# Expert stages of a four-layer block: pad rows and expert sums spread over other slots, and the loads of the sums issued six slots later

## The reference

```python
probs = softmax(x @ gate_weight.T)                 # 32 experts
top_vals, top_idx = top_k(probs, 8)
rw = top_vals * (cumsum(renormed top_vals) < 0.8)  # at most 7 of the 8 are kept
rw = rw / sum(rw)
for each expert e:
    g, u = split(x @ gate_up[e].T)                 # 256 -> 2 * 96
    out += (silu(g) * u) @ down[e].T * share_of_e  # 96 -> 256
```

## Time and profile before

| what | value |
|---|---|
| median of the runs shown | 1091.12 us |
| the profiled execution | 1090.43 us |
| its span, first to last instruction | 1088.7 us |
| TensorE busy | 877.9 us, 81% |
| GpSimd busy | 642.1 us, 59% |
| VectorE busy | 583.0 us, 54% |
| ScalarE busy | 544.2 us, 50% |
| mean granted TensorE clock | 0.911 of full speed |

### The profile page before, as it was taken

How to read it: one execution, slowest core, us unless ns; L and a number is a source line. 1 busy time by engine, 2 the same in 40 slices (tenths; PEclk the granted TensorE clock), 3 DMA queues, 4 the chain that set the end, 5 groups by cost and what they waited for, 6 DMA issues and landing times. The chain is left out here.

```text
span 1088.7 us, 20645 instructions
## 1 busy us (share of the span) xinstructions
PE 877.9 (81%) x5504; PEld 665.9 (61%) x5504; DVE 583.0 (54%) x2104; ACT 544.2 (50%) x1084; POOL 642.1 (59%) x636
## 2 busy tenths in 40 slices
PE   5999998971489899999368998988758998999940
PEld 4666665641388699998233443544327887999830
DVE  4566785775373222226776488765535522222665
ACT  6333446640145455555268776766423554556520
POOL 2466648787577777775730010373754777777770
PEclk9999999995599999999679998988887999999975
DMA  9600002162578887773540110135326888778776
GB/s 335 252 1 2 1 20 91 67 240 78 168 233 301 281 267 220 222 259 123 174 136 35 34 35 35 49 121 215 116 103 200 261 303 280 227 218 255 270 243 204
DMA packets 93231, 181.64 MB, mean 167 GB/s; under 512 B 18985, under 2 KB 73788, under 8 KB 92736
## 3 DMA queue, kind: packets, MB, share of 16 engines
q1 hardware_dynamic: 68544, 114.19, 32.7%
q0 software_dynamic: 24576, 66.13, 16.7%
HBM read 96.34 MB, written 92.27 MB: 173 GB/s over the span
## 5 line engine op out<-in xcount | busy, mean ns | idle before, releaser
L1304 POOL DMA_INDIRECT result_rows<-ys,result_slots x288 | 286.6, 995 | 88.0 <-issue 81.0
L989 POOL DMA_INDIRECT expert_rows<-route_rows,index x224 | 223.0, 996 | 87.1 <-issue 68.0
L1955 ACT ACTIVATE b_probs<-ps 128x1024 f32<-128x1024 f32 x128 | 127.9, 1031 | 42.7 <-PE ps L1804 42.1
L1456 PE MATMUL ps<-w_gu,f_xts 128*128 x576 | 107.7, 331 | 3.3 <-ACT f_xts L1499 2.9
L1456 PE MATMUL ps<-w_gu,g_xts 128*128 x576 | 107.6, 330 | 2.9 <-ACT g_xts L1499 2.1
L1456 PEld LDWEIGHTS ps<-w_gu,f_xts 128*128 128x128 f32 x576 | 93.6, 193 | 4.5 <-issue 4.4
L1456 PEld LDWEIGHTS ps<-w_gu,g_xts 128*128 128x128 f32 x576 | 93.4, 193 | 4.3 <-issue 4.1
L1816 PE MATMUL ps<-b_probs,b_v_pad 128*32 128x512 f32 x512 | 78.4, 688 | 11.5 <-issue 5.4
L1549 DVE SCALAR_TENSOR_TENSOR g_h<-ps,g_xs,g_gate 128x96 f32<-128x96 f32 x144 | 39.1, 313 | 90.6 <-ACT g_gate L1506 87.7
L1549 DVE SCALAR_TENSOR_TENSOR f_h<-ps,f_xs,f_gate 128x96 f32<-128x96 f32 x144 | 39.2, 313 | 89.4 <-ACT f_gate L1506 88.3
L1517 ACT COPY ys<-ps 128x512 f32<-128x512 f32 x144 | 83.5, 580 | 1.9 <-PE ps L1475 1.9
(11 more groups left out here) (362 smaller groups left out, 1824.6 us busy)
## 6 DMA issues: line engine op xcount, KB each, us to landing
parts<-result_rows SPq DMA_DIRECT2D x32, 896.0 KB, 4.8
f_xs<-expert_rows SPq DMA_DIRECT2D x144, 160.0 KB
g_xs<-expert_rows SPq DMA_DIRECT2D x144, 160.0 KB
expert_rows<-pad_rows SPq DMA_DIRECT2D x64, 160.0 KB
w_gu<-in_Wgu SPq DMA_DIRECT2D x1, 6144.0 KB, 18.7
expert_rows<-pad_rows SPq DMA_DIRECT2D x1, 5120.0 KB, 29.9
result_rows<-ys,result_slots POOLq DMA_INDIRECT x288, 3.1
f_w_d<-in_Wdown SPq DMA_DIRECT2D x1, 4096.0 KB, 15.3
```

Of the source, the lines that this page charges most:

```text
L989: self.nc.gpsimd.indirect_dma_start(xs, bass.IndirectOffsetOnAxis(self.index[:, f, t, r:r + 1].bitcast(U32), 0), self.x_rows(f)[:, t, :], ...
L1304: self.nc.gpsimd.indirect_dma_start(self.y_dram, bass.IndirectOffsetOnAxis(self.slots[:, i, j:j + 1].bitcast(U32), 0), self.ys[:, i, j, :] ...
L1456: ins = nc.tensor.matmul(ps[:, bank_gu[u % 2], j * GU:(j + 1) * GU], xts[:, u % 2, o:o + P], w_gu[:, k, bass.ds(experts[j] * GU, GU)], sta ...
L1955: nc.scalar.activation(probs[:, u % RING, :, :], ps[:, 2 * (u % 2):2 * (u % 2) + 2, :], ACT.Exp, scale=float(HD) ** -0.5).then_inc(exp_don ...
```

## The change

Five things are edited.

1. Pad stores: they begin in SyncE's slot 11 instead of 17 and stand in every second slot (11, 13, ... 25) instead of every slot (17 to 24). The table of their rows is now computed in routing step 12 (slot 3), with a semaphore `padded` of its own, instead of step 16 (slot 8).
2. Sums of stage one: tiles 0 to 7 in slots 56, 58, ... 70. Attention's preparation sums none, and attention loads results from tile 8 on.
3. Sums of stage two: tile t in slot 55 + 2t, so 55 to 85.
4. Result loads: `loads_at(u)` is now `sums_at(u - 6)`. The load of a tile stands in SyncE's slot number six higher than its sum in VectorE's: 62 to 76 in stage one, 61 to 91 in stage two.
5. Slot 0: TensorE and ScalarE do their routing steps before pair 0. In stage two GpSimd scatters the results of pairs 0 and 1 in slot 4, before the token rows of the last batch.

```diff
-    PADS_AT = 17
+    PADS_AT = 11
     PADS = 4
+    PADS_EVERY = 2
...
                 if first == 0:
-                    routing.wait_tiles(sp, LAST)
+                    sp.wait_ge(routing.padded, 1)
...
-                if PADS_AT <= u < PADS_AT + E // PADS:
-                    store_pads(PADS * (u - PADS_AT), PADS)
+                nth = (u - PADS_AT) // PADS_EVERY
+                if (u - PADS_AT) % PADS_EVERY == 0 and 0 <= nth < E // PADS:
+                    store_pads(PADS * nth, PADS)
...
             held = {}
             wait_weights(pe)
+            for step, f in steps_at(0):
+                routing.tensor(pe, step, f, bank_route, apart=True)
...
-                for step, f in steps_at(u):
+                for step, f in steps_at(u) if u > 0 else ():
                     routing.tensor(pe, step, f, bank_route, apart=True)
...
-            sums = {-1: {9: 4, 16: 5, 26: 6, 30: 7}, 0: {1: 8, 3: 9, 13: 10, 28: 11}, 1: {13: 12, 23: 13, 27: 14, 31: 15}}
+            sums = {0: {1: 8, 3: 9, 13: 10, 28: 11}, 1: {13: 12, 23: 13, 27: 14, 31: 15}}
...
-            for t in range(TT, NT):
+            for t in range(2 * TT, NT):
...
+        def early_pairs(scattered):
+            return 2 if (Routing.ALL - scattered) // 2 <= placed + 1 else 0
+
         def results_at(u, scattered, last):
 
-            left = (Routing.ALL - scattered) // 2
+            left = max((Routing.ALL - scattered) // 2, placed)
             pairs = TILES // 2 if last else TILES // 2 - LATER
-            if u == max(left, placed) + Routing.ALL // 2:
-                for v in range(pairs):
+            early = early_pairs(scattered)
+            if u == left - 1:
+                for v in range(early):
                     yield v
+            if u == left + Routing.ALL // 2:
+                for v in range(early, pairs):
+                    yield v
 
         def sums_at(u, last):
 
-            first, count = (62, NT) if last else (66, TT)
+            first, count = (55, NT) if last else (56, 2 * TT)
             at = u - first
             if at >= 0 and at % 2 == 0 and at // 2 < count:
                 yield at // 2
+
+        def loads_at(u, last):
+
+            return sums_at(u - 6, last)
```

More of the change, by code:

```diff
@@ L954, in __init__ @@
         self.chosen_ready, self.pos_ready, self.index_ready = sem("chosen_ready"), sem("pos_ready"), sem("index_ready")
-        self.counted, self.listed = sem("counted"), sem("listed")
+        self.counted, self.listed, self.padded = sem("counted"), sem("listed"), sem("padded")
         self.scattered = [sem(f"scattered{f}") for f in range(B)]
@@ L1153, in vector @@
                                     ALU.add).then_inc(self.index_ready, 1)
+            if f == B - 1:
+                dve.wait_ge(self.counted, f + 1)
+                nc.vector.tensor_scalar(self.pads[:, :], self.count[:, 0, :], -1.0, None, ALU.add).then_inc(self.padded, 1)
         self.vec_n = steps.n
@@ L1253, in list_tiles @@
             steps(nc.vector.tensor_tensor(self.row[:, :], self.row[:, :], self.valid[:, :], ALU.add))
-            if final:
-                steps(nc.vector.tensor_scalar(self.pads[:, :], self.count[:, 0, :], -1.0, None, ALU.add))
-            else:
+            if not final:
                 steps(nc.vector.tensor_scalar(flat(self.used), flat(self.since), -1.0, float(tiles), ALU.mult, ALU.add))
@@ L1339, in experts @@
     FLUSH = 4
-    PADS_AT = 17
+    PADS_AT = 11
     PADS = 4
+    PADS_EVERY = 2
+    assert PADS_AT + PADS_EVERY * (E // PADS - 1) < (TILES - PHASES[-1][1]) // 2
     LOADED = [COVERED[sum(t >= n for n in (2 * TT, 3 * TT, 3 * TT + TT // 2))] // 2 for t in range(NT)]
@@ L1518, in keep_result @@
                                ps[:, bank_y[u % 2], :].rearrange("p (j n) -> p j n", j=2)).then_inc(y_ready, 1)
+            for step, f in steps_at(0):
+                routing.scalar(act, step, f, bank_route)
             for u in range(PAIRS + FLUSH):
@@ L2292, in program @@
                         lambda u: scatters_at(u, scattered), lambda u: results_at(u, scattered, final),
-                        lambda u: sums_at(u, final), lambda u: sums_at(u, final), out_rows if final else None,
+                        lambda u: loads_at(u, final), lambda u: sums_at(u, final), out_rows if final else None,
                         weights_ready(use))
```

## The result

The changed kernel takes 1138.2 us (median of 4 runs, 1133.9 to 1140.1) against 1090.4 us for the kernel before (4 runs beside them, 1088.1 to 1091.2): 1.0439 times as long, 95% interval 1.0411 to 1.0466. The profiled span went from 1088.7 to 1138.3 us, in executions of 1090.4 and 1140.0 us. Two executions further down were slow ones, at 1516.6 us (of the kernel before) and 4730.7 us (of pads_at9), and count in no ratio.

The account below looks back on a forecast made before the run. TensorE was taken to set the pace of both expert stages. Stage one +26.4, preparation -2 and stage two +16.8 gave +41.2 us, so 1132 us, with a range of 1114 to 1150.

Parts of the forecast that it names:

- The loop: Expert stages: issue 1.6, landing 6.0, sum 2.6, gate step 1.2 make 11.4 us per two pairs, costing 5.75 us a tile.
- a deeper queue can't catch it up: Expert stages: the time lost to late result loads can't be caught up with a deeper queue; no size given.
- First sums: Start of each stage's sums: the first result load also waits for 88 scatters; +4.9 us stage one, +4.4 stage two.
- the gain is not kept: Stage one: the pads' gain counts as nothing, since load 0 is held until pair 43's scatters land at 465.6 us.
- The way out: After the loops in each stage: -1.5 us for TensorE's lead over the gate step, an estimate between 0 and 2.82.
- the clock falls too: Rival: idle TensorE in the loops lowers its clock, some 4 us a stage lost on the way out; 1140 us, 13%.
- The pad waits go: -7.5 and -7.8 us: Pad stretches of stages one and two: pads in every second slot remove the waits, -7.5 and -7.8 us.
- Slot 0: Start of each stage: pair 0 now follows the router's work, +0.9 us a stage, covered by the hold on load 0.
- Preparation: Attention's preparation without four sums: -2 us, taken from between 0 and 2 x 2.6 us.
- The end: After the last gate step: seven sums instead of eleven, 4 x 3.7 = -14.9 us; GpSimd's backlog doesn't bind.
- the loads arrive in time: Rival: the kernel gets faster; stage one -6.6, preparation -2, stage two -6.9 and -14.9, about 1061 us; 5%.

Follow-up runs that it names:

- pads_at9: sums_back with the pads in slots 9 to 23 instead of 11 to 25; 1083.0 us (0.9938 of the kernel before).
- ring9: The changed kernel with nine instead of eight buffers in the ring of pair loads; 1093.3 us (1.0028 of the kernel before).
- sums_back: The changed kernel with sums, their loads and attention's table as in the kernel before; 1081.6 us (0.9913 of the kernel before).
- sums_alone: The kernel before with only the sums and their loads changed, attention's part included; 1145.9 us (1.0518).
- pads_alone: The kernel before with the pads edit alone; 1083.7 us (0.9942).
- slot0_alone: The kernel before with the slot 0 edit alone; 1092.2 us (1.0022).
- late3: The changed kernel with loads three slots behind their sums' number and first sums in slots 59 (stage one) and 58 (stage two); 1077.8 us (0.9897).

## Why the prediction was right, point by point

**The loop: right mechanism, each turn too short.** Forecast 11.4 us for two pairs, measured 12.2 in stage one (48.8 us for four turns) and 12.0 in stage two (60.1 us for five). The term that was mis-sized in stage one is the landing: from issue to fold the looping loads took 5.5 to 7.6 us, 6.75 on average in stage one and 6.15 in stage two, where I took 6.0. In stage two the landing is 0.15 us of the excess; the way from gate step to load took 1.8 us for a forecast of 1.6, and that from fold to gate step 4.0 for 3.8. My reason for going under the stage's median of 6.4, that fewer pair loads run beside it, was wrong: two pairs' loads go out in 12 us, but one pair's stand just ahead of each result load and the other's 1.1 to 2.0 us behind it. The mean over the nine turns is 6.4, the median I had. The loops took 6.2 us more than forecast. The other misses are 4.3 us on the way out and 2 in the preparation, against 4.1 us by which the first sums and the end came out lower; together that is the 8.4 us between +41.2 and +49.6. Tiles in the loop: 0 to 4 and 0 to 5, as forecast. That a deeper queue can't catch it up was wrong, as ring9 shows (1093.3 us).

**First sums.** +3.5 and +2.6 us instead of +4.9 and +4.4. The step that failed is "the gain is not kept": load 0 was not held in stage one and by about 2.4 us in stage two. Two terms were off. The pads gained less than I had counted, so that pair 54's gate step ended at 461.3 us and not at 458; and the 88th scatter of stage one started at 460.7 us, not 462.4, and landed 2.5 us later instead of 3.2. In stage two it started 157.6 us after pair 0's gate step for a forecast of 159.0, the microsecond for the early scatters already counted in, and landed after 3.0. That made the forecast a few microseconds too high, the opposite way from the miss. sums_back and sums_alone show that the parts add to within some 3 us, so the pads were worth most of their gain here too.

**The way out.** I subtracted 1.5 us a stage for TensorE's lead; the traces give +1.1 and +0.2 instead. Why there is no such lead at the end of the loop stays open. The granted clock was 0.77 to 0.80 in the loops and 0.66 from 520 to 530 us, so the rival "the clock falls too" is true as to the clock; its price of 4 us a stage isn't seen, at most 2.6 and 1.7 us between forecast and measurement, and no run separates clock and lead. The Trainium skill's rule that I cited, "TensorE: Matmul & The Clock Gate", section "Why this matters for your kernels", agrees with these rows: one wait of 2.6 to 6.7 us in each turn between the bursts, and a lower clock.

**Pads.** Spread as they are, the waits went only in part, 5.0 of 8.3 us in stage one and 7.6 of 9.1 in stage two. The step that erred is "The pad waits go: -7.5 and -7.8 us": I counted SyncE's backlog and left out that pair 26 waits for the last pads' landing, which the edit puts right ahead of it. Nor did I count that pairs 0 to 10 of stage one get slower by about 1 us.

**Slot 0.** Forecast +0.9, covered. In the changed kernel pair 10's gate step of stage one does come 0.9 us later, counted from pair 0's (33.2 us, 32.3 before). But pads_alone, without the slot 0 edit, has the same 33.2 us, and slot0_alone 32.5. The size was right by luck, the cause was not.

**Preparation.** -2 can't be told. From pair 71's gate step to pair 0's of stage two, six traces with the four sums there give 316.7 to 319.5 us (mean 318.2), eight without them 313.8 to 321.0 (mean 317.0). The difference of 1.1 is within the spread of 7 us.

**The end.** -15.8 for a forecast of -14.9, because the slow stage gave GpSimd time: the last scatter ended at 1119.2 and tile 14's load went out only at 1124.05. The rival "the loads arrive in time" at 1061 us was out of reach for a reason that the prediction names only for the slow case: with timely loads GpSimd's scatters bind. late3, whose loads are in time and whose sums begin three slots later, takes 1077.8 us.

## What to carry to other kernels

A slot number says where an instruction stands in its own queue, not when it runs: measure how far two queues are apart (here SyncE runs eight pairs ahead, held by its ring), subtract the offset, and compare what is left with a landing. The cost is a cliff, not a slope, when the late load sits ahead of the very loads that feed the pipeline: one pair of lead was worth 43 us here. And before moving work out of a tail, look for who is next to bind there; an engine whose queue hardly pauses through a stage, as GpSimd's, sets a floor that its busy share of the whole span, 59% before the change, doesn't show.

## What the runs showed of the hardware

- An 896 KB result load took 5.5 to 7.6 us beside pair loads in the loop and 4.8 to 5.5 us at the end, after the last pair, from issue to fold. The Trainium skill's estimate for another issuing path ("DMA: Bandwidth & Descriptors", section "Anatomy of one DMA — SWDGE (gpsimd) path"), 4.1 us, was met by none of the changed kernel's loads; the least was 4.3 us from issue to landing.
- Eight sums beside the pairs of stage two cost TensorE nothing when their data is there: in late3 it is busy for 39.99 of 40 us from 997 to 1037 us at clock 1.00, with VectorE busy for 28.9.
- Four stores of pad rows, issued by SyncE by 367.04 us, had all landed at 370.5 us in the changed kernel, 3.5 us later.
- GpSimd's scatters of 128 result rows start 1.28 us apart when nothing holds them: 0.97 us each and 0.30 between.
- Attention, untouched but for its first part, varied by 7 us from trace to trace; profiles of single executions can't tell a change of 2 us there.
